# ScalarE's exp stands behind the square of q and the copy of P's transposes

## The chip, the cores and the metric

The kernel runs on one core of a Trainium2 chip. The time is the device time of the core in microseconds, the median of repeated runs. Five engines work side by side, each with its own queue in program order, and wait for each other by semaphores: TensorE (PE in the profile), VectorE (DVE), ScalarE (ACT), GpSimd (POOL) and SyncE (SP), which starts the DMAs.

## The reference, cut to what matters

The input is 16 sequences of 256 tokens with 128 features. A first stage adds a windowed attention with 16 heads of 8. Then come six layers, each an attention and a feed-forward part:

```
for i in range(6):
    x = attn_layer(shift_tokens(x), Wqkv[i], q_scale[i], k_scale[i], Wo[i]) + x
    x = ffn_layer(shift_tokens(x), ln_g[i], ln_b[i], W1[i], b1[i], W2[i], b2[i]) + x

# attn_layer: 16 heads of 64, windows of 32 queries that see 64 keys
q, k, v = split(x @ Wqkv)
q, k = l2norm(q) * qs, l2norm(k) * ksc       # then rotary tables on both
sim = q @ k.T * 8, masked;  attn = softmax(sim);  out = (attn @ v) @ Wo
```

`l2norm` needs the sum of squares of each head of q and k. The softmax needs a row maximum, exp, a row sum and a division.

## The kernel before, in words

After the first stage the six layers run as one software pipeline over blocks of 128 tokens: 32 blocks a layer, 192 in all. In step t every engine does one stage of several blocks at once. Block t (back 0) is projected, squared and rotated. Block t-1 has its q and k transposed and its scores computed. Block t-2 has its maximum, its shift, exp and row sum. Block t-3 has its probabilities P transposed, multiplied with v and projected. Block t-4 is added to x. The feed-forward part of a pair of blocks (a sequence) goes along, split over later steps: `pl.seq(9)` and `pl.seq(11)` act at odd t, `pl.seq(6)` and `pl.seq(10)` at even t. Each engine's order within a step is written out by hand in `step_pe`, `step_act`, `step_dve`, `step_pool` and `step_sp`; nothing reorders it, except that steps of all engines overlap as their semaphores allow.

**TensorE, step t:** q projection into the bank pair `one` (six fp32r matmuls, `q_done`); eight transposes of P of block t-3 into `PC` (waits for `weighed` and for `x_updated` of t-4; `pT_done`); k projection into `other` (`k_done`); eight q transposes of block t-1 into `PC` (wait for `pT_kept`; `qkT_done`); P times v of block t-3 into `PB` (waits for `pT_kept` and `shifted`; `av_done`); eight k transposes of block t-1, into `PC` again (wait for `qkT_kept`, that is for the two copies of qT at L855); v projection; the feed-forward matmuls; scores of block t-1 into `PB`, on top of a mask that VectorE wrote (`masked`); the output projection of t-3.

**ScalarE, step t:** exp of block t-2 in place in `Sx` (L832, waits for `shifted`); square of q into `sq[:, 0]` (L837, waits for `q_done`); copy of P's transposes into `PT` (L840, waits for `pT_done`); square of k into `sq[:, 1]` (L845, waits for `k_done`); at even t a small bias (L850); two copies of qT (L855); oT (L860); kT (L865); VA (L872); then the feed-forward and normalization parts.

**VectorE, step t:** maximum (L998) and shift (L1002) of the scores of t-2; the update of `xT` from t-4 (L1006, `x_updated`); rotation of q in two multiplications (L973, L977; waits for the first `squared`); sums of the squares of q (L981); rotation of k (waits for the second `squared`); the mask for the next scores (L994, waits for `o_kept`, the oT copy); sums of the squares of k; row sums of exp (L1029, waits for `exp_done`) and their reciprocal (L1032); feed-forward parts. GpSimd adds the halves of the rotation (L1101), scales q and k by their norms (L1080) and divides the probabilities (L1112).

At the turn from one layer to the next, VectorE and ScalarE also prepare the next layer's weights and tables. TensorE's projections are interspersed with counts of a semaphore that nobody waits for (`fill`).

Of the kernel before, what the change touches and what calls it, by code (L numbers as in the profile page):

```python
# [9 lines left out]
ACT = mybir.ActivationFunctionType  # L10
# [59 lines left out]
def build(nc, x_in, w_first, wqkv, wo, qkscale, fw1, fw2, vectors, c_rot, c_small, out):  # L70
    ctx = ExitStack()
    with ctx:
        def sb(name, shape, dt=F32):
            return ctx.enter_context(nc.sbuf_tensor(name, shape, dt))

        def sem(name):
            return ctx.enter_context(nc.semaphore(name))
# [38 lines left out]
        Sx = sb("Sx", [P, 2, PAIRS, 2, KEYS])  # L116
# [39 lines left out]
        S = {n: sem(n) for n in (*STEP, *PER_SEQ, *LOADS, *PARTS, *ONCE, *FIRST, "xf0", "xf1", "vb0", "vb1", "vb2", "vb3", "phase",   # L156
                                 "stored", "opened", "o_copied", "o_t", "o_sum", "zeroed",
                                 "cleared", "waited")}
# [48 lines left out]
        A_ = nc.scalar  # L207
# [387 lines left out]
        def blocks(pl, name, back, k):  # L595

            per = STEP[name]
            return pl.times(NBLOCKS * per) + ((pl.t - back) * per + k)
# [57 lines left out]
        def feed_banks(t):  # L656

            other = projections(t)[1]
            return other[:, 0:UNIT], other[:, UNIT:2 * UNIT], PC[:, UNIT:2 * UNIT]
# [165 lines left out]
        def step_act(e, pl):  # L825
            t, r, b, now = pl.t, pl.t % RING, pl.t % BLOCKS, pl.t % 2
            one, other = projections(t)
            bank0, bank1, bank2 = feed_banks(t)
            if pl.has(2):
                e.wait_ge(S["shifted"], blocks(pl, "shifted", 2, 1))  # L830
                rows = Sx[:, now, :, :, :].rearrange("p a w k -> p (a w k)")
                A_.activation(rows, rows, ACT.Exp).then_inc(S["exp_done"], 1)  # L832
            if pl.has(0):
                e.wait_ge(S["q_done"], blocks(pl, "q_done", 0, 1))
                if pl.has(1):
# [2 lines left out]
            if pl.has(3):  # L838
                e.wait_ge(S["pT_done"], blocks(pl, "pT_done", 3, 1))
                A_.activation(PT[:, :, :].rearrange("p a q -> p (a q)"), PC[:, :], ACT.Copy).then_inc(S["pT_kept"], 1)  # L840
            if pl.has(0):
                e.wait_ge(S["k_done"], blocks(pl, "k_done", 0, 1))
                if pl.has(1):
                    e.wait_ge(S["summed"], blocks(pl, "summed", 1, 2))
                A_.activation(sq[:, 1, :], other[:, :], ACT.Square).then_inc(S["squared"], 1)  # L845
# [5 lines left out]
            if pl.has(1):  # L851
                e.wait_ge(S["qkT_done"], blocks(pl, "qkT_done", 1, 1))
                for odd in range(2):
                    rows = slice(odd * DH, (odd + 1) * DH)
# [403 lines left out]
        @block.scalar  # L1258
        def _(act):
            act.wait_ge(S["zeroed"], 1)  # L1260
            A_.preload_act_table_set("natural_log_exp_and_others")
            first = Place(act, 0).at(0)
            act.wait_ge(S["w_loaded"], 16)
            act.wait_ge(S["v_cleared"], 1)
            first_stage(act, first_act)
            meet(act, 1)
            act.wait_ge(S["cleared"], 1)
            for q in range(2):
                round_x(act, first, q)
            steps(act, step_act)  # L1270
            meet(act, 2)
            finish(act, "act")
# [64 lines left out]
```

## Time and profile before

| | |
|---|---|
| median of 3 runs | 3418.71 us (3418.09 to 3419.04) |
| profiled execution | 3418.27 us, span 3416.5 us |
| granted TensorE clock, mean | 0.973 |
| TensorE matmuls busy | 3188.8 us, 93% |
| VectorE busy | 2812.1 us, 82% |
| GpSimd busy | 2626.1 us, 77% |
| ScalarE busy | 2597.2 us, 76% |

Times are microseconds from the start of the span unless marked ns. A row of a timeline gives start, length, engine, line, operation, output from input; in brackets stands the idle time of the engine just before it and what ended it. Lengths of pipelined instructions overlap: the pitch, from start to start, is what a queue pays. The chain of waits is followed back from the last instruction of the kernel: it names, at each moment, the work that everything later waited for.

### The profile page before, as it was taken

Reading aid. Unit: us, or ns where it says so; the run is one execution under the profiler, and the core shown is the slowest. Engines: PE = TensorE matmul, PEld = TensorE weight load, DVE = VectorE, ACT = ScalarE, POOL = GpSimd, SP = SyncE. Lnnn points to the kernel's source line nnn. Section 1 sums busy time; section 2 is a strip of 40 time slices with the busy share of each in tenths; the row PEclk is TensorE's granted clock in tenths of the full one; section 3 lists DMA queues with packets and bytes.
Section 4 is the critical chain, followed back from the end, with each engine's and each line's share of the span. In section 5 each row is a group of like instructions: output and inputs, shape, how many; then the busy total and the mean of one; then the engine's idle time right before and its main releaser. Section 6 shows DMA issues by size and latency. Waiting matters only on the chain.

```text
span 3416.5 us, 133004 instructions
## 1 busy us (share of the span) xinstructions
PE 3188.8 (93%) x52802; PEld 2706.0 (79%) x52802; DVE 2812.1 (82%) x3743; ACT 2597.2 (76%) x3707; POOL 2626.1 (77%) x2593
## 2 busy tenths in 40 slices
PE   7978999989999989999989999989999999999996
PEld 4647888878788878888878888878888878888885
DVE  7967888888788888888888888888878888888882
ACT  6746778877787878778777877878778777878874
POOL 6648888878877878878878878877878887888871
PEclk9979999999999999999999999999999999999997
DMA  1001111111111111111101111111111111111111
GB/s 63 2 10 36 58 39 33 38 28 44 52 43 38 35 31 41 43 56 35 40 27 46 36 58 39 33 33 39 40 59 33 38 35 38 37 40 33 38 35 29
DMA packets 57827, 130.82 MB, mean 38 GB/s; under 512 B 10992, under 2 KB 33136, under 8 KB 56432
## 3 DMA queue, kind: packets, MB, share of 16 engines
q1 hardware_dynamic: 57200, 121.94, 12.2%
q8 instruction: 457, 7.49, 0.9%
q14 instruction: 170, 1.39, 0.1%
HBM read 19.17 MB, written 2.10 MB: 6 GB/s over the span
## 4 chain that ended last, share of the span: by engine, by line
PE 70%; ACT 15%; issue 8%; DVE 5%; POOL 2%; ACTq 0%; DMA 0%; POOLq 0%; DVEq 0%; SPq 0%
PE pair L211 56%; PE pair L214 13%; ACT qT L855 10%; ACT sq L845 3%; DVE ts L977 1%; ACT ss L850 1%; DVE ss L981 1%; DVE mx L998 1%; DVE qk L973 0%; DVE pair L994 0%; DVE tab L955 0%; POOL qk L1080 0%; DVE tab L956 0%; DVE Sx L1002 0%; ACT sq L837 0%
## 5 line engine op out<-in xcount | busy, mean ns | idle before, releaser
L1101 POOL TENSOR_TENSOR qk<-qk,ts 128x1024 f32<-128x1024 f32 x384 | 912.4, 2385 | 228.8 <-DVE ts L977 213.5
L973 DVE TENSOR_TENSOR qk<-pair,tab 128x1024 f32<-128x1024 f32 x384 | 468.2, 1219 | 365.6 <-ACT sq L837 362.8
L1080 POOL TENSOR_TENSOR qk<-qk,rn 128x1024 f32<-128x1024 f32 x384 | 733.1, 1930 | 28.6 <-issue 13.5
L211 PE MATMUL pair<-wq_h,xs_h 128*128 128x512 f32 x1154 | 512.3, 444 | 31.6 <-issue 14.8
L832 ACT ACTIVATE Sx<-Sx 128x1024 f32<-128x1024 f32 x192 | 203.4, 1060 | 395.4 <-DVE Sx L1002 395.4
L214 PE MATMUL pair<-small,qk 128*128 128x128 f32 x3104 | 420.5, 279 | 75.4 <-ACT qT L855 54.5
L1112 POOL TENSOR_TENSOR Sx<-Sx,rden 128x1024 f32<-128x1024 f32 x192 | 365.3, 1902 | 157.2 <-DVE rden L1032 157.2
L211 PE MATMUL pair<-wq_h,xs_l 128*128 128x512 f32 x1152 | 469.7, 408 | 0.4
L211 PE MATMUL pair<-wq_l,xs_h 128*128 128x512 f32 x1152 | 468.4, 407 | 0.0
L977 DVE TENSOR_TENSOR ts<-pair,tab 128x1024 f32<-128x1024 f32 x384 | 466.0, 1214 | 0.0
L981 DVE TENSOR_REDUCE ss<-sq 128x16 f32<-128x1024 f32 x384 | 463.9, 1208 | 0.0
L214 PEld LDWEIGHTS pair<-small,qk 128*128 128x128 f32 x3104 | 338.0, 143 | 154.7 <-issue 106.1
L211 PEld LDWEIGHTS pair<-kT,qT 128*64 128x64 f32 x12288 | 374.4, 138 | 36.2 <-issue 36.2
L211 PE MATMUL pair<-kT,qT 128*64 128x64 f32 x12288 | 400.6, 224 | 2.2 <-DVE pair L994 1.9
L855 ACT ACTIVATE qT<-pair 64x1024 f32<-64x1024 f32 x384 | 389.3, 1014 | 8.0 <-PE pair L214 5.1
L211 PE MATMUL pair<-oT,wo_sb 128*128 128x128 f32 x3072 | 394.5, 282 | 0.0
L211 PE MATMUL pair<-PT,VB 64*64 64x32 f32 x12288 | 375.6, 221 | 5.5 <-issue 3.1
L211 PE MATMUL pair<-PT,VA 64*64 64x32 f32 x12288 | 371.8, 220 | 0.6 <-issue 0.6
L211 PEld LDWEIGHTS pair<-oT,wo_sb 128*128 128x128 f32 x3072 | 358.3, 192 | 12.8
L211 PEld LDWEIGHTS pair<-PT,VB 64*64 64x64 f32 x12288 | 327.5, 135 | 36.5 <-issue 36.4
L211 PEld LDWEIGHTS pair<-PT,VA 64*64 64x64 f32 x12288 | 328.5, 135 | 2.1 <-issue 2.1
L214 PE MATMUL pair<-small,Sx 128*128 128x128 f32 x1792 | 246.5, 283 | 49.2 <-DVE xT L1006 39.7
(126 smaller groups left out, 6678.6 us busy)
## 6 DMA issues: line engine op xcount, KB each, us to landing
VB<-VA SPq DMA_DIRECT2D x192, 384.0 KB, 3.5
VB<-VA SPq DMA_DIRECT2D x96, 128.0 KB, 3.5
wq_raw<-wqkv SPq DMA_DIRECT2D x6, 1536.0 KB, 7.2
xf<-xT SPq DMA_DIRECT2D x96, 64.0 KB, 1.9
xf<-xT SPq DMA_DIRECT2D x96, 63.8 KB, 2.0
wo_sb<-wo SPq DMA_DIRECT2D x6, 512.0 KB, 3.6
X<-x_in SPq DMA_DIRECT2D x4, 512.0 KB, 7.6
out<-X SPq DMA_DIRECT2D x8, 256.0 KB, 2.3
```

The source lines that it names most:

```text
L211: return T_.matmul(out, lhsT, rhs, start=start, stop=stop, **k)
L214: return T_.transpose(out, in_, ident if idn is None else idn)
L832: A_.activation(rows, rows, ACT.Exp).then_inc(S["exp_done"], 1)
L845: A_.activation(sq[:, 1, :], other[:, :], ACT.Square).then_inc(S["squared"], 1)
L850: A_.activation(ss[:, 2 * HEADS:NORMS], f_mv[:, :, 1], ACT.Identity, bias=eps[:, 0:1]).then_inc(S["varied"], 1)
L855: last = A_.activation(qT[rows, :, :, odd * WIN:(odd + 1) * WIN], PC[rows, :].rearrange("p (a w q) -> p a w q", a=PAIRS, w=4), ACT.Copy)
L973: V_.tensor_tensor(h3(qk[:, now, kind, :], DH), h3(source[:, :], DH), rep(tab[:, 2 * kind, b, :], HEADS, DH), ALU.mult)
L977: V_.tensor_tensor(ts[:, kind, :].rearrange("p (h a c) -> p h a c", **halves), swapped, sines, ALU.mult).then_inc(S["rotated"], 1)
L981: V_.tensor_reduce(ss[:, kind * HEADS:(kind + 1) * HEADS], h3(sq[:, kind, :], DH), axis=AX.X, op=ALU.add).then_inc(S["summed"], 1)
L1080: G_.tensor_tensor(x, x, bc(rn[:, then, kind * HEADS:(kind + 1) * HEADS], HEADS, DH), ALU.mult).then_inc(S["scaled"], 1)
L1101: G_.tensor_tensor(qk[:, now, kind, :], qk[:, now, kind, :], ts[:, kind, :], ALU.add).then_inc(S["added"], 1)
L1112: G_.tensor_tensor(x, x, bc(rden[:, now, :], HEADS, KEYS), ALU.mult).then_inc(S["weighed"], 1)
```

## The change: ScalarE's order in a step

The exp of block t-2 moves down by two instructions. ScalarE now squares q first, then copies P's transposes, then does exp, and then squares k. All waits and counts of the semaphores stay as they are, and so does the order of every other engine.

```diff
--- before.py
+++ after.py
@@ -826,10 +826,6 @@
             t, r, b, now = pl.t, pl.t % RING, pl.t % BLOCKS, pl.t % 2
             one, other = projections(t)
             bank0, bank1, bank2 = feed_banks(t)
-            if pl.has(2):
-                e.wait_ge(S["shifted"], blocks(pl, "shifted", 2, 1))
-                rows = Sx[:, now, :, :, :].rearrange("p a w k -> p (a w k)")
-                A_.activation(rows, rows, ACT.Exp).then_inc(S["exp_done"], 1)
             if pl.has(0):
                 e.wait_ge(S["q_done"], blocks(pl, "q_done", 0, 1))
                 if pl.has(1):
@@ -838,6 +834,10 @@
             if pl.has(3):
                 e.wait_ge(S["pT_done"], blocks(pl, "pT_done", 3, 1))
                 A_.activation(PT[:, :, :].rearrange("p a q -> p (a q)"), PC[:, :], ACT.Copy).then_inc(S["pT_kept"], 1)
+            if pl.has(2):
+                e.wait_ge(S["shifted"], blocks(pl, "shifted", 2, 1))
+                rows = Sx[:, now, :, :, :].rearrange("p a w k -> p (a w k)")
+                A_.activation(rows, rows, ACT.Exp).then_inc(S["exp_done"], 1)
             if pl.has(0):
                 e.wait_ge(S["k_done"], blocks(pl, "k_done", 0, 1))
                 if pl.has(1):
```

## Rows read from the trace of the kernel before

**Rows 1.** The page: busy time and share of each engine; the chain by line.

```profile
PE 3188.8 (93%) x52802; PEld 2706.0 (79%) x52802; DVE 2812.1 (82%) x3743; ACT 2597.2 (76%) x3707; POOL 2626.1 (77%) x2593
...
PE pair L211 56%; PE pair L214 13%; ACT qT L855 10%; ACT sq L845 3%; DVE ts L977 1%; ACT ss L850 1%; DVE ss L981 1%; DVE mx L998 1%; DVE qk L973 0%; DVE pair L994 0%; DVE tab L955 0%; POOL qk L1080 0%; DVE tab L956 0%; DVE Sx L1002 0%; ACT 
```

**Rows 2.** The chain in order of time (start, length, what), 1500 to 1535.

```profile
1507.93 1.43 PE pair L211 x6
...
1509.46 1.02 ACT sq L845
...
1511.40 1.03 ACT qT L855
...
1512.57 1.07 PE pair L214 x8
...
1516.78 5.39 PE pair L211 x86
```

**Rows 3.** The table of waits: us in total, times, the longest.

```profile
DVE qk L973 <- ACT sq L837: 362.8, 192, 6.7
...
PE pair L214 <- ACT qT L855: 54.5, 189, 2.2
...
PE pair L214 <- DVE xT L1006: 39.7, 6, 8.0
```

**Rows 4.** ScalarE's timeline, 1500 to 1535: start, length, line, operation.

```profile
1507.20 1.00 ACT L837 ACTIVATE sq<-pair 128x1024 f32<-128x1024 f32 x1
1508.11 1.02 ACT L840 ACTIVATE PT<-pair 128x1024 f32<-128x1024 f32 x1
1509.46 1.02 ACT L845 ACTIVATE sq<-pair 128x1024 f32<-128x1024 f32 x1 [0.34 <-PE pair L211]
...
1512.45 1.03 ACT L860 ACTIVATE oT<-pair 128x1024 f32<-128x1024 f32 x1
...
1521.83 1.06 ACT L832 ACTIVATE Sx<-Sx 128x1024 f32<-128x1024 f32 x1 [2.19 <-DVE Sx L1002]
1522.80 1.01 ACT L837 ACTIVATE sq<-pair 128x1024 f32<-128x1024 f32 x1
1523.70 1.01 ACT L840 ACTIVATE PT<-pair 128x1024 f32<-128x1024 f32 x1
1524.87 1.03 ACT L845 ACTIVATE sq<-pair 128x1024 f32<-128x1024 f32 x1 [0.16 <-PE pair L211]
```

**Rows 5.** TensorE's timeline, the same stretch.

```profile
1506.66 0.39 PE L211 MATMUL pair<-wq_l,xs_h 128*128 128x512 f32 x1
1506.89 1.03 PE L214 MATMUL pair<-small,Sx 128*128 128x128 f32 x8
...
1508.95 0.40 PE L211 MATMUL pair<-wq_l,xs_h 128*128 128x512 f32 x1
...
1521.78 0.39 PE L211 MATMUL pair<-wq_l,xs_h 128*128 128x512 f32 x1
1522.23 1.09 PE L214 MATMUL pair<-small,Sx 128*128 128x128 f32 x8
...
1524.33 0.43 PE L211 MATMUL pair<-wq_l,xs_h 128*128 128x512 f32 x1
```

**Rows 6.** VectorE's timeline, the same stretch.

```profile
1508.24 1.23 DVE L973 TENSOR_TENSOR qk<-pair,tab 128x1024 f32<-128x1024 f32 x1 [1.84 <-ACT sq L837]
...
1513.90 1.22 DVE L994 COPY pair<-small 128x1024 f32<-128x1024 f32 x1
...
1521.71 0.28 DVE L1006 TENSOR_TENSOR xT<-pair,xT 128x128 f32<-128x128 f32 x1
```

**Rows 7.** Weight loads in time, 1686 to 1688.

```profile
1687.20 0.19 PEld L211 LDWEIGHTS pair<-f_h,w_h 128*128 128x128 f32 x1 [0.45 <-issue]
```

**Rows 8.** The chain in order of time, 1262 to 1269, at a layer turn.

```profile
1264.80 2.29 PE pair L211 x6
```

**Rows 9.** Busy time by stretch (count), then PEclk, DMA share, GB/s.

```profile
50.00:100.00 50.00, 45.57 (x566) 30.47 (x564) 47.12 (x109) 37.74 (x102) 34.93 (x80) 1.00 0.01 2
```

## The prediction

> **What bounds the kernel now.** I began with the page: TensorE is the busiest engine at 93%, and in the chain of waits its two lines hold 56% and 13% [rows 1]. So TensorE sets the pace, with one detour through ScalarE: qT L855 is 10% of the chain and sq L845, the square of k, 3%. VectorE, busy for 82%, has no line above 1% in it.
>
> The chain in order of time shows that detour [rows 2]. TensorE ends the k projection, ScalarE squares k (from 1509.46), then makes the two qT copies, and only then does TensorE start the k transposes at 1512.57. The table of waits says the same of nearly every block: TensorE waited for qT 189 times [rows 3]. It shows only 54.5 us for this, but a wait that sits in the chain matters by being last, not by its length: whatever makes qT later makes TensorE later by as much.
>
> Then I laid out a pair of blocks from the timelines, one odd t (first instruction of the changed region at 1507.20) and one even t, and measured everything from Q, the end of the q projection. For the odd block Q = 1506.66 + 0.39 = 1507.05, for the even one 1521.78 + 0.39 = 1522.17 [rows 5].
>
> - Odd block: square of q at Q + 0.15, P copy at Q + 1.06, square of k at Q + 2.41 [rows 4]. The k projection ends at 1508.95 + 0.40 = 1509.35, Q + 2.30 [rows 5]. So the square of k starts 0.11 after its matmuls end: nothing but that latency holds it.
> - Even block: exp at 1521.83, square of q at Q + 0.63, P copy at Q + 1.53, square of k at Q + 2.70 [rows 4], with the k projection ending at 1524.33 + 0.43 = 1524.76, Q + 2.59 [rows 5]. Again 0.11 of latency.
>
> In both, ScalarE reaches the square of k with time to spare, because exp ran ahead of Q, while ScalarE had nothing else to do. VectorE waits too, 1.84 us before its rotation [rows 6] and 362.8 us in all [rows 3], for the square of q. That wait looks like the prize of this change, but VectorE hardly stands in the chain.
>
> **The change, part by part.** No instruction is added or removed; 192 exps move past the square of q and the P copy, and land right before the square of k. No DMA is moved, and nothing on TensorE, VectorE or GpSimd changes its place. Two new queueing relations arise: exp now waits behind q_done and pT_done, and the square of k waits behind exp.
>
> The square of q. It waits for q_done alone and starts at about Q + 0.11 (the latency seen at the square of k). Gain: 0.04 in the odd block, 0.52 in the even one. It goes to VectorE's rotation and to the P copy.
>
> The P copy. It comes 0.91 after the square of q (1507.20 to 1508.11 [rows 4]), so at Q + 1.02. In the odd block the transposes of P run from 1506.89 for 1.03 and are done by Q + 0.87 [rows 5]: in time. In the even block they start 0.45 after the last q matmul instead of 0.23 [rows 5], right after VectorE's xT update, which runs from 1521.71 for 0.28 [rows 6]. VectorE gains 0.5 on TensorE here (below), so I take this 0.22 gap as closed, and the copy at Q + 1.02 too.
>
> exp. The pair "P copy, then exp" doesn't stand in this trace. Bounds: a pitch of 0.91, that of the square of q and the P copy, and 1.05 if nothing overlaps, as from the second qT copy at 1511.40 [rows 2] to oT at 1512.45 [rows 4]. Two pairs overlap by 0.09: the square of q lasts 1.00 with a pitch of 0.91, exp lasts 1.06 with a pitch of 0.97. So I take 1.02 - 0.09 = 0.93 for the P copy, nearest to them in shape and line: exp at Q + 1.95.
>
> The square of k. It follows an exp by 0.97 (1521.83 to 1522.80 [rows 4]): Q + 2.92. Its matmuls end at Q + 2.30 in the odd block and, with the gap closed and the P copy earlier, near that in the even one. So exp is now what it waits for, in both blocks. It is later by 2.92 - 2.41 = 0.51 in the odd block and 2.92 - 2.70 = 0.22 in the even one. Other even blocks, read in the same way, have it up to Q + 2.81, and there 0.11 is lost. I use 0.18 as the mean.
>
> Behind it on ScalarE stand qT (both halves), oT, kT and VA. qT goes straight into TensorE's wait for the k transposes, so all of TensorE's later work in the block (k transposes, v projection, feed-forward part, scores, output projection, next q projection) moves by the same 0.51 or 0.18. oT is needed by VectorE's mask copy at 1513.90, Q + 6.85 [rows 6]. oT begins at Q + 5.40 now [rows 4]; at Q + 5.91 and 1.03 long it holds the mask until about Q + 7.0, some 0.15 late. But the scores, which read it, follow the short transposes at 1516.78, Q + 9.7 [rows 2], so the mask stays covered, and VectorE still gains about 0.5 - 0.15 on TensorE in the odd block: this closes the 0.22 gap of the even one. exp's own readers lose nothing: the row sums stand behind the mask in VectorE's order, and the mask starts 4 us after exp's new end.
>
> The sum. The first blocks have no P copy or exp, and at the five layer turns the k projection runs at half clock, 2.29 us for its six matmuls instead of 1.43 [rows 8, 2], which covers exp. That leaves about 95 odd blocks at 0.51 = 48.5 and 88 even ones at 0.18 = 16: 64.5 us. Some even blocks have stalls in TensorE's own stream after the k transposes: weights that wait 0.45 for "issue" [rows 7]. I take a part, 3 us, as absorbed there, since a longer wait ahead of them may let the queue fill. Total +61.
>
> The profiled execution took 3418.27 us, span 3416.5, and the median of the runs is 3418.71. They agree within 0.5, so I add the sum to the median: 3480 us.
>
> **Rivals.**
>
> *Half of the move (faster).* If TensorE could use the earlier P copy and the square of q, the even block would lose its 0.22 gap and about 0.2 ahead of the q transposes (they start 0.53 after the last k matmul there, 0.32 in the odd block). Up to 0.4 x 90 = 36 us faster, 3383. This needs exp to fit in before the k projection ends, that is, the projection would have to end at Q + 2.80 or later. For it: VectorE's 362.8 us of waiting. Against: it ends at Q + 2.30 in the odd block. 4%.
>
> *Hidden anyway (same).* If TensorE's wait for qT weren't last, or the later stalls of its queue absorbed 0.2 to 0.5 in each block, the time would stay at 3419. Against: the chain passes through qT in both blocks, and odd blocks show no such stall behind it. 4%.
>
> *Worse bounds (slower still).* No overlap between P copy and exp (+0.12 x 183 = 22), and the even block's 0.22 gap stays because it is TensorE's queue and not xT (+0.22 x 88 = 19): 3480 + 41 = 3521; either alone gives about 3500. 17% for something near both, 3505 to 3525.
>
> *The clock.* The longer stall, up to 0.8 us per block where 54.5 / 189 = 0.29 stands now [rows 3], might cost TensorE its clock. The granted clock is 1.00 (of 2.4 GHz) from 50 to 100 us, where TensorE is busy 45.57 of 50 us, 91% [rows 9]. It was at 1.2 GHz behind the one long wait of a turn, 8.0 us for xT [rows 3, 8]. After the change TensorE would be busy 3189 of some 3478 us, 92%: above that first stretch. If in a fifth of the blocks the k transposes and the v projection, 1.07 and about 1.4 us, took twice as long, that is 0.2 x 2.5 x 192 = 96 us more, 3576. The Trainium skill's "TensorE: Matmul & The Clock Gate", section on psum-queue depth-cycling, reports a kernel whose micro-idles between groups of matmuls made the clock oscillate; by that rule this rival would come true. The trace of before has short idles in every block and the full clock over the stretch of [rows 9], so it doesn't agree so far. 3%.
>
> **How the numbers follow.** Forecast 72%, worse bounds 17%, clock 3%, faster 4%, same 4%. A difference of 0.2% (7 us) is about what can be told from no change. Most of the range is the forecast's own bounds. It goes down to 3456, where the start latency is 0.07 instead of 0.11, the even blocks lose nothing and the turns give back about half of VectorE's 1.84 (-7, -13, -4), and up to 3508, which takes in either of the worse bounds alone. Slower 0.92, same 0.04, faster 0.04.
>
> **What would show it.** After the change: exp at Q + 1.95, the square of k at Q + 2.9 in both blocks with a releaser on ScalarE itself instead of the k projection; TensorE's wait for qT up from 54.5 to about 54.5 + 60 and more (up to 120, since the closed gaps reappear there); VectorE's wait before L973 for sq L837 down, but idle before L998 (for the scores) up; the xT-bound gap in even blocks gone; ScalarE idle before L837 instead of before exp. The prediction is wrong if the square of k still starts 0.11 after its matmuls, or if the odd block's period, 15.12 us from Q to Q now, doesn't grow by about 0.5.

## The result and the profile after

The changed kernel takes 3478.4 us (median of 4 runs, 3475.05 to 3483.91) against 3418.88 before: a ratio of 1.0173, 95% interval 1.0156 to 1.0191. It is slower by about 59.5 us; 3480 was forecast, with 3456 to 3508 as the range. The profiled execution took 3475.05 us, its span is 3473.3.

The page's chain, by line:

```profile
PE pair L211 50%; ACT qT L855 10%; PE pair L214 9%; ACT sq L845 5%; ACT sq L833 5%; ACT PT L836 5%; ACT Sx L840 2%; ACT ss L850 1%; DVE wq_l L963 0%; DVE tab L955 0%; POOL sq L399 0%; DVE VB L321 0%; POOL wq_l L963 0%; DVE qk L317 0%; DVE m
```

Three ScalarE instructions are new in it: sq L833 (the square of q), PT L836 (the P copy) and Sx L840 (exp). Before, the chain touched ScalarE only from the square of k on [rows 2]; now the whole row from the square of q to qT stands in it. The chain in order of time, in an odd block:

```profile
1555.30 1.03 ACT sq L833
1556.33 0.92 ACT PT L836
1557.24 0.30 ACT Sx L840
...
1558.07 1.02 ACT sq L845
1559.10 0.89 ACT qT L855
```

ScalarE's timeline, an even block and the odd one behind it:

```profile
1538.93 1.03 ACT L833 ACTIVATE sq<-pair 128x1024 f32<-128x1024 f32 x1 [2.65 <-PE pair L211]
1539.91 1.03 ACT L836 ACTIVATE PT<-pair 128x1024 f32<-128x1024 f32 x1
1540.97 1.06 ACT L840 ACTIVATE Sx<-Sx 128x1024 f32<-128x1024 f32 x1
1541.94 1.01 ACT L845 ACTIVATE sq<-pair 128x1024 f32<-128x1024 f32 x1
...
1555.30 1.03 ACT L833 ACTIVATE sq<-pair 128x1024 f32<-128x1024 f32 x1 [2.09 <-PE pair L211]
1556.22 1.02 ACT L836 ACTIVATE PT<-pair 128x1024 f32<-128x1024 f32 x1
1557.12 1.06 ACT L840 ACTIVATE Sx<-Sx 128x1024 f32<-128x1024 f32 x1
1558.07 1.02 ACT L845 ACTIVATE sq<-pair 128x1024 f32<-128x1024 f32 x1
```

TensorE's, the same stretch:

```profile
1538.43 0.39 PE L211 MATMUL pair<-wq_l,xs_h 128*128 128x512 f32 x1
1538.79 1.09 PE L214 MATMUL pair<-small,Sx 128*128 128x128 f32 x8
...
1545.20 1.06 PE L214 MATMUL pair<-small,qk 128*128 128x128 f32 x8 [0.84 <-ACT qT L855]
...
1554.79 0.39 PE L211 MATMUL pair<-wq_l,xs_h 128*128 128x512 f32 x1
...
1557.08 0.40 PE L211 MATMUL pair<-wq_l,xs_h 128*128 128x512 f32 x1
...
1561.16 1.06 PE L214 MATMUL pair<-small,qk 128*128 128x128 f32 x8 [0.71 <-ACT qT L855]
```

In the odd block Q = 1554.79 + 0.39 = 1555.18. The square of q starts at Q + 0.12, the P copy at Q + 1.04, exp at Q + 1.94, the square of k at Q + 2.89, though its matmuls ended at Q + 2.30. Against [rows 4] that is 0.48 later. In the even block Q = 1538.82: Q + 0.11, 1.09, 2.15 and 3.12, where the square of k stood at Q + 2.70. TensorE's idle before the k transposes, 0.23 to 0.24 before, is 0.71 and 0.84 now. Over all blocks the medians for the square of k are Q + 2.89 (2.40 before) in odd blocks and Q + 3.12 (2.75 before) in even ones. The odd block's period, which was to grow by about 0.5 from 15.12, is 15.59 in the block before this one (Q = 1523.23 to 1538.82): 0.47 more.

The table of waits, against [rows 3]:

```profile
ACT sq L833 <- PE pair L211: 494.6, 191, 8.3
DVE qk L973 <- ACT sq L833: 336.1, 187, 6.8
...
PE pair L214 <- ACT qT L855: 139.6, 190, 2.2
```

TensorE waits 85 us more for qT. VectorE's wait for the square of q shrank by only 27 us, from 362.8: its rotation can start no earlier than TensorE's q projection allows, and it now waits for oT too. The 395.4 us that ScalarE used to idle ahead of exp are 494.6 us of idling ahead of the square of q: the room in which exp ran unseen is still there, and nothing stands in it.

By blocks, from one kT copy to the next on ScalarE's timeline: the 164 steady blocks (from t = 12 on, without the blocks around the turns) take 63.6 us more, 0.39 each; the 15 blocks at the turns 2.3; the first 12 together 0.1. The first stage, in which no instruction differs, happened to be 6.4 shorter, and the end 2.7. Together 56.8, the difference of the spans.

### The profile page after: what moved, and what is told of

Its sections match the earlier page's. It is cut to its first block, busy times and chain, and to the rows that moved or that the text cites. A ratio compares the mean times of both kernels' runs of the same rounds, so it can differ in the third digit from the quotient of the medians.

```text
span 3473.3 us, 133004 instructions
## 1 busy us (share of the span) xinstructions
PE 3169.9 (91%) x52802; PEld 2700.4 (78%) x52802; DVE 2829.9 (81%) x3743; ACT 2586.7 (74%) x3707; POOL 2625.7 (76%) x2593
## 4 chain that ended last, share of the span: by engine, by line
PE 59%; ACT 29%; issue 7%; DVE 3%; POOL 1%; ACTq 0%; DMA 0%; DVEq 0%; POOLq 0%; SPq 0%
PE pair L211 50%; ACT qT L855 10%; PE pair L214 9%; ACT sq L845 5%; ACT sq L833 5%; ACT PT L836 5%; ACT Sx L840 2%; ACT ss L850 1%; DVE wq_l L963 0%; DVE tab L955 0%; POOL sq L399 0%; DVE VB L321 0%; POOL wq_l L963 0%; DVE qk L317 0%; DVE mx L998 0%
## 5 line engine op out<-in xcount | busy, mean ns | idle before, releaser
L833 ACT ACTIVATE sq<-pair 128x1024 f32<-128x1024 f32 x192 | 196.9, 1025 | 494.6 <-PE pair L211 494.6
L214 PE MATMUL pair<-small,qk 128*128 128x128 f32 x3104 | 419.6, 278 | 155.9 <-ACT qT L855 139.6
L211 PEld LDWEIGHTS pair<-wq_h,xs_h 128*128 128x128 f32 x1154 | 222.6, 193 | 74.9 <-issue 26.7
```

What stands on the lines that cost most here:

```text
L211: return T_.matmul(out, lhsT, rhs, start=start, stop=stop, **k)
L214: return T_.transpose(out, in_, ident if idn is None else idn)
L833: A_.activation(sq[:, 0, :], one[:, :], ACT.Square).then_inc(S["squared"], 1)
```

## Experiments

Ratios are against the kernel before on the same chip, whose median was 3414.74 us in the first four runs, 3420.5 in the next four, 3416.62 in the last four. Orders name ScalarE's instructions of a step: q and k for the squares, P for the copy, E for exp; before is E q P k qT oT kT VA, after is q P E k qT oT kT VA. Q is the end of the q projection throughout. Two theories stood at the start: mine, that an instruction costs by what TensorE waits for behind it (here qT); and that exp being late, or VectorE's order of waits, costs by itself. The diffs are shortened: words in place of code stand for one ScalarE instruction or more, "..." for what is left out. Where a median over blocks is given for an experiment, it is that of the steady blocks of its profiled execution, 89 odd and 83 even ones from t = 15 on, without the even blocks at the turns.

**1. exp one place up (q E P k).**

```diff
             (square of q)
+            exp of t-2
             (copy of P)
-            exp of t-2
             (square of k)
```

> ScalarE's order is square of q, exp, copy of P, square of k: exp moves one place up from the changed kernel. The square of k should stand at Q + 2.9 as in the changed kernel. My theory (TensorE waits for qT, and qT waits for whatever stands before it or for the q transposes, which need the P copy): P copy from Q + 1.1 to about Q + 2.0, the q transposes start at its end + 0.14 = Q + 3.15 and end at Q + 4.2, qT can start only then, some 0.45 later than in the changed kernel: 3478 + 0.42 x 180 = about 3553 us. Rival (only that exp stands somewhere ahead of the square of k counts): 3478, no change.

Measured 3548.06 us, ratio 1.039 (1.0373 to 1.0407). The chain in time, odd block, from the square of q:

```profile
1553.43 1.02 ACT sq L833
1554.46 0.95 ACT Sx L837
1555.41 0.92 ACT PT L840
...
1556.46 1.08 PE pair L214 x8
...
1557.57 1.02 ACT qT L855
...
1559.76 1.06 PE pair L214 x8
```

The square of k starts at 1556.21 with Q = 1552.92 + 0.40 = 1553.32, the same Q + 2.9 as after, yet the kernel is some 70 us slower. The P copy holds the q transposes, these hold qT, which starts at Q + 4.25, 0.46 later than in the changed kernel. So it isn't the square of k as such, nor exp's distance from it: it is when qT can start.

**2. exp behind the square of k (q P k E qT).**

```diff
             (square of k)
+            exp of t-2
             (bias L850, even blocks)
             (copies of qT)
```

> Order square of q, copy of P, square of k, exp, qT. The square of k goes back to 0.11 after the k projection (Q + 2.4 odd, Q + 2.6 to 2.7 even). My theory (qT's start is what counts): exp now holds qT by its whole pitch of 0.97 with no slack ahead to absorb it, so 3419 + 0.97 x 95 + 0.9 x 88 less 10 for the turns = about 3575 to 3590 us. Rival (the late square of k itself costs, through VectorE's rotation of k and the sums): 3410 to 3419 us.

Measured 3655.16 us, ratio 1.0706 (1.0688 to 1.0724). ScalarE, odd block (qT follows at 1634.66):

```profile
1632.79 1.02 ACT L841 ACTIVATE sq<-pair 128x1024 f32<-128x1024 f32 x1 [0.35 <-PE pair L211]
1633.71 1.05 ACT L845 ACTIVATE Sx<-Sx 128x1024 f32<-128x1024 f32 x1
```

The square of k is back at 0.1 after its matmuls and the time is the worst of all: the rival is out. But 240 us is 69 to 84 more than the 156 to 171 that I expected. TensorE's idle for qT is mostly 1.18 to 1.44 a block here, and behind some of these idles the clock falls: cut into 140 stretches of 20 us from 400 to 3200, the trace has 58 with a granted clock below 1.00; before there are 15, after 14. Summed as (1 - clock) x 20 us, what is missing to full clock is 112 us here, 39 before and 41 after: some 71 us more than after, about the size of the excess. The next run shows the same effect coming in.

**3. A small copy ahead of the square of k, in both kernels.**

```diff
+            if pl.has(0):
+                A_.activation(junk[:, :], small[:, 0:256], ACT.Copy)
             if pl.has(0):
                 e.wait_ge(S["k_done"], ...)
```

> The changed kernel with one more ScalarE copy of 128x256 into a tile that nobody reads, right before the square of k (pitch about 0.33 to 0.40 by the small copies of this kernel). My theory: no slack is left there, so every block pays it whole: 3478 + 0.36 x 183 = 3540 to 3550 us. Rival (the time came from somewhere else, VectorE's new order of waits or TensorE's queue, and ScalarE still has slack before the square of k): 3478 to 3485 us.

> The same copy at the same place in the kernel before. There the slack before the square of k is 2.41 - (1.06 + 0.93) = 0.42 in odd blocks and 2.70 - (1.53 + 0.93) = 0.24 in even ones. My theory: odd blocks pay nothing, even ones about 0.1: 3419 to 3432 us. Rival (any work added to ScalarE costs its length): 3419 + 66 = 3485 us.

Measured in the changed kernel 3559.85 us, ratio 1.0411 (1.0386 to 1.0437): 81 us more than without it. In the kernel before 3418.06 us, ratio 1.0014 (1.0003 to 1.0025): 3 to 5 us. ScalarE in the kernel before with the copy, an odd block:

```profile
1540.37 1.02 ACT L841 ACTIVATE PT<-pair 128x1024 f32<-128x1024 f32 x1
1541.28 0.42 ACT L843 ACTIVATE junk<-small 128x256 f32<-128x256 f32 x1
1541.72 1.03 ACT L848 ACTIVATE sq<-pair 128x1024 f32<-128x1024 f32 x1
```

and in the changed one:

```profile
1565.47 1.06 ACT L841 ACTIVATE Sx<-Sx 128x1024 f32<-128x1024 f32 x1
1566.41 0.41 ACT L843 ACTIVATE junk<-small 128x256 f32<-128x256 f32 x1
1566.72 1.02 ACT L848 ACTIVATE sq<-pair 128x1024 f32<-128x1024 f32 x1
```

The copy, 0.42 long, just fits ahead of the square of k in the first and pushes it by its pitch of 0.31 in the second. The same work at the same place costs next to nothing in one order and all of its pitch in the other; that is the slack that the change used up. Its 81 us are more than 0.31 x 183 = 57. The rest sits in blocks where TensorE ran at 1.2 GHz: 32 of the 140 stretches are below 1.00, and by the same sum 70 us are missing to full clock, 28 more than after. Such a block:

```profile
1551.96 1.66 PE L215 MATMUL pair<-small,qk 128*128 128x128 f32 x8 [1.19 <-ACT qT L858]
...
1553.84 0.63 PE L212 MATMUL pair<-wq_h,xs_l 128*128 128x512 f32 x1
1554.27 0.63 PE L212 MATMUL pair<-wq_l,xs_h 128*128 128x512 f32 x1
```

Eight k transposes take 1.66 instead of 1.06, and the fp32r matmuls stand 0.43 apart instead of 0.23, right behind an idle of 1.19. Counted over all blocks, no such group was slow behind the 153 waits for qT of 0.6 to 0.9 us in the changed kernel; with the copy added 9 of 131 were behind idles of 0.9 to 1.1, and in the run of experiment 2 13 of 93 behind 1.1 to 1.3 and 33 of 83 behind longer ones.

**4. exp further down, where ScalarE has time: behind kT, oT, VA.** exp is gone from its place ahead of the square of q in all three.

```diff
             (copies of qT)
             (copy oT)         + exp here: behind oT
             (copy kT)         + exp here: behind kT
             (copy VA)         + exp here: behind VA
```

> Order square of q, copy of P, square of k, qT, oT, kT, exp, VA: exp goes where ScalarE waits for the v projection anyway (0.45 idle), and nothing of TensorE's next waits stands behind it but VA. My theory: the square of k is back at 0.11 after the k projection, Q + 2.4 odd and about Q + 2.6 even (2.75 before), exp ends at about Q + 8.6 (odd) and Q + 9.1 (even), just ahead of VectorE's row sums; the turns keep their 2 us each: 3415 - 9 - 10 = about 3395 to 3405 us, faster than both. Rival (exp late is what costs, through row sums and division): 3430 us and more.

> exp between oT and kT. The square of k and qT as in the run with exp behind kT, but kT ends about 0.75 later, Q + 8.4 in odd blocks, and there TensorE's transposes of xf into the same bank wait for it (they start at Q + 7.8 in the kernel before). My theory (each instruction's place is priced by the wait of TensorE that stands behind it): odd blocks lose about 0.6, even ones nothing: 3400 + 57 = 3455 us or so. Rival (only work ahead of qT costs): 3400 us.

> exp behind VA, at Q + 9.1 to 9.6, ending at Q + 10.1 to 10.6. VectorE's row sums stood at Q + 9.1 before and now wait for it, about 1.0 to 1.5 a block, and VectorE has some 1.7 us of waiting per block elsewhere, but its maximum for the next block comes late. My theory: VectorE's lateness reaches TensorE through x_updated at the next transposes of P, 0.3 to 0.8 a block: 3450 to 3550 us. Rival (VectorE's slack swallows it): 3400 us.

Measured: behind kT 3428.61 us, ratio 1.0026 (1.0016 to 1.0037); behind oT 3496.98 us, 1.0235 (1.022 to 1.0251); behind VA 3546.89 us, 1.0379 (1.0363 to 1.0396).

Behind kT 50 of the 59 us are back, with exp later still. From the table of waits of that run:

```profile
DVE hid L1066 <- ACT hid L894: 125.8, 103, 9.7
...
DVE den L1029 <- ACT Sx L865: 8.6, 2, 7.6
```

VectorE's row sums waited for exp only twice, so being late isn't what costs there, though the rival's 3430 us is nearer than my 3400. It isn't faster than before either, and three other things differ, whose shares I didn't separate. In an even block VectorE's xT update ends at 1523.19, the transposes of P start at 1523.43, 0.46 after the last q matmul, and the square of k stands at Q + 2.72: the gap of 0.22 is back, because VectorE gains on TensorE only when TensorE is slower. In 50 of the 83 even blocks xT sets the start in this way, and the median for the square of k is Q + 2.71, not the 2.6 that I expected. Next, the bias L850 follows the square of k by 1.05 in even blocks, where it was 0.92 before, and qT starts at Q + 3.96 (3.84 before, medians). And the gelu parts stand behind exp on ScalarE now: VectorE waits 125.8 us for them (63.9 before), and in 37 of the 89 odd blocks the transposes of P start late, behind xT, which happened in none before.

Behind oT the chain goes through kT, as expected, and costs more than I worked out:

```profile
1504.56 0.22 ACT Sx L861
...
1505.40 1.03 ACT kT L865
...
1506.57 0.41 PE pair L214 x2
```

kT from 1505.40 ends at 1506.43, and TensorE's transposes of xf follow 0.14 later. From kT to kT, against the kernel before, odd blocks take 0.72 more (57.5 us for 80 of them; 0.6 was expected), and a part of the even blocks another 22.6 us, which I did not follow up. Behind VA exp's lateness itself is on the path, through VectorE's row sums and on to xT, as I expected (3450 to 3550 us), and VectorE's slack doesn't swallow it. Its table of waits:

```profile
DVE den L1029 <- ACT Sx L873: 246.8, 192, 8.0
...
PE pair L214 <- DVE xT L1006: 132.3, 138, 5.4
```

VectorE waits 246.8 us for exp, TensorE 132.3 us for xT (39.7 before).

**5. Fewer counting instructions between TensorE's matmuls, in even blocks.** The transposes of P in even blocks start 0.36 after the last q matmul in the changed kernel, with xT ready at 1537.97 + 0.28 = 1538.25, 0.54 ahead.

```diff
-        FILL = (43, 21, 46, 21, 44, 22, 47, 21, 46, ...)
+        FILL = (21, 21, 21, 21, 21, 22, 21, 21, 21, ...)
```

> The changed kernel, in which the counting instructions strewn over TensorE's projections are about 21 in every block, where even blocks had 39 to 48. In the changed kernel the transposes of P in even blocks start 0.36 to 0.39 after the last q matmul although xT was ready 0.5 before; in odd blocks 0.23. If TensorE's instruction queue makes this gap (my theory now), it falls to 0.23, the P copy comes 0.1 earlier, exp overlaps it as in odd blocks, and the square of k goes from Q + 3.12 to Q + 2.89 in even blocks: 3478 - 0.23 x 85 = about 3458 us. Rival (the gap has another cause): no change, 3478; moved fetches of instructions at the loop's turn may add or take a few us in either case.

Measured 3473.84 us, ratio 1.0169 (1.0153 to 1.0184), not to be told from the changed kernel's 1.0173. An even block on TensorE:

```profile
1539.86 0.40 PE L211 MATMUL pair<-wq_l,xs_h 128*128 128x512 f32 x1
1540.10 1.03 PE L214 MATMUL pair<-small,Sx 128*128 128x128 f32 x8
```

and on ScalarE:

```profile
1541.29 1.02 ACT L836 ACTIVATE PT<-pair 128x1024 f32<-128x1024 f32 x1
1542.34 1.06 ACT L840 ACTIVATE Sx<-Sx 128x1024 f32<-128x1024 f32 x1
```

The gap is gone, as my theory said: 0.24 in this block, at most 0.26 in 71 of the 83 even blocks, and 0.23 in the median, where the changed kernel has 0.37. So the counts made it. But the gain of 20 us didn't follow, for two reasons. exp still starts 1.05 after the P copy and not 0.90, so the square of k comes at Q + 3.05 (median; 3.12 in the changed kernel, 2.89 expected). And the counts aren't idle decoration: TensorE now stops for about 0.8 us of "issue" in the middle of the matmuls of P with v in 40 blocks, 4 in the changed kernel. The period of even blocks fell from 16.48 to 16.35 (medians), while that of odd ones rose from 15.60 to 15.69 (means).

**6. The bias L850 (even blocks, pitch 0.19) moved from ahead of qT to ahead of kT, in three kernels.**

```diff
             (square of k)
-            (bias L850)
             (copies of qT)
             (copy oT)
+            (bias L850)
             (copy kT)
```

> The changed kernel with the small bias of even blocks (L850, pitch 0.19) moved from ahead of qT to between oT and kT, where ScalarE idles 0.19. My theory (in the changed kernel ScalarE's row from the square of q to qT is the chain, with no gap): even blocks win 0.19, 3478 - 0.19 x 85 = about 3462 us. Rival (ScalarE has room before qT): 3478 us.

> The same move in the kernel before. There the q transposes end at Q + 3.78 in even blocks and qT starts at Q + 3.81, so qT would wait for TensorE instead: my theory says 3415 to 3420 us, no change. Rival (the whole row ahead of qT is the chain there too): 3420 - 16 = 3404 us.

> The run with exp behind kT, with the bias moved too. There the q transposes end at about Q + 3.6 in even blocks, qT starts at Q + 3.97: the move can win 0.3 a block: 3428 - 0.3 x 85 = about 3403 us, which would be faster than the kernel before by 0.4%. Rival (what made that run slower than 3400 lies behind the k transposes): 3425 us.

Measured: in the changed kernel 3465.59 us, ratio 1.0139 (1.0124 to 1.0155), by the ratios 12 us less than without the move, with intervals that just touch, and the period of even blocks fell by 0.14 (medians 16.48 and 16.34); in the kernel before 3420.63 us, 1.0009 (1.0 to 1.0018), nothing won; with exp behind kT 3417.24 us, 0.9998 (0.9989 to 1.0007), 10 us less by the ratios, not the 25 that I expected. The first two are the pair of experiment 3 with the sign turned: taking 0.19 away from ScalarE's row pays where the row is the chain, and not where it has slack.

The third is level with the kernel before, not faster. VectorE and TensorE at its even to odd seam:

```profile
1529.29 1.26 DVE L1066 SCALAR_TENSOR_TENSOR hid<-pair,vec_b,hid 128x256 f32<-128x256 f32 x3 [1.11 <-ACT hid L894]
...
1532.86 0.28 DVE L1006 TENSOR_TENSOR xT<-pair,xT 128x128 f32<-128x128 f32 x1
```

```profile
1533.05 0.39 PE L211 MATMUL pair<-wq_l,xs_h 128*128 128x512 f32 x1
1533.38 1.09 PE L214 MATMUL pair<-small,Sx 128*128 128x128 f32 x8
```

exp ahead of VA delays VA and with it, on ScalarE, the table load and the gelu parts of even blocks. VectorE waits 1.11 for them, its xT update ends at 1533.14, and the odd block's transposes of P start 0.24 after that, 0.33 after the last q matmul instead of 0.23. 38 of the 89 odd blocks start them late, none before. Against the kernel before, the period of even blocks is 0.09 shorter (medians 16.05 and 15.96) and that of odd ones 0.10 longer (15.11 and 15.21): what the even block wins, the odd one gives back.

**7. The square of q one place down (E P q k).**

```diff
             exp of t-2
-            (square of q)
             (copy of P)
+            (square of q)
             (square of k)
```

> Order exp, copy of P, square of q, square of k: the kernel before with the square of q one place down. The square of k then stands at about Q + 2.8 odd and Q + 3.1 even, as in the changed kernel, but the square of q comes at Q + 1.9 to 2.2 instead of Q + 0.11. If TensorE's wait for qT alone sets the price and VectorE's 1.7 us of waiting is slack: 3478 us. My theory now: VectorE has 11.1 us of work between its rotation and its maximum in an odd block, it would end 1.8 later, more than its slack, and TensorE would wait for xT: 3600 us or more.

Measured 3584.64 us, ratio 1.0488 (1.0472 to 1.0504), far from 3478 and somewhat under my figure. VectorE's waits:

```profile
DVE qk L973 <- ACT sq L840: 655.2, 192, 6.7
...
PE pair L214 <- ACT qT L855: 114.3, 179, 2.2
...
PE pair L214 <- DVE xT L1006: 87.2, 86, 2.1
```

VectorE's wait for the square of q grows from 362.8 to 655.2 us. TensorE's rise for qT is only 60 us of the 168; it now also waits for xT in 86 places, 6 before, as I expected. In even blocks the transposes of P start 1.40 after the last q matmul (0.45 before), and they hold the P copy and with it the squares: the square of q stands at Q + 3.05 and that of k at Q + 3.95 there, far behind the 3.1 that I expected, so these blocks aren't those of the changed kernel with a late square of q alone. So the square of q can't be late; no run here shows a gain from its being early.

## Why the prediction was right

**The mechanism.** The runs bear it out: TensorE waits for qT behind a row of ScalarE's work, exp filled an idle stretch ahead of Q, and moved behind Q it used up the slack ahead of the square of k (0.42 in odd blocks, 0.24 in even ones) and then pushed qT. qT came 0.47 later in odd blocks (Q + 3.79, 3.32 before) and 0.36 later in even ones (4.20, 3.84 before). Experiment 3 shows the slack, 1 and 2 show that qT's start counts and not the square of k, 4 that exp's lateness does not count until it meets the row sums.

**Odd blocks, 0.51 forecast.** The square of k came at Q + 2.89, forecast Q + 2.92. Start latency 0.12 (0.11), q to P 0.92 (0.91), P to exp 0.90 (0.93), exp to k 0.95 (0.97).

**Even blocks, 0.18 forecast: too small.** The square of k came at Q + 3.12, not 2.92, so 0.37 later than its median before. The step that failed is "I take this 0.22 gap as closed". VectorE gained what I worked out, xT was ready 0.5 ahead, yet the gap shrank only from 0.45 to 0.36. And the P copy and exp don't overlap there: 1.06 from start to start, the "no overlap" bound of the range, where odd blocks have 0.90. Experiment 5 shows what I had wrong: xT was one bound of that gap, and the counting instructions of even blocks, which the sum put at nothing, were the next one, at 0.37 in the median. With fewer of them the gap is 0.23. Why exp doesn't overlap the P copy in even blocks stays open.

**What evened it out.** The terms at 0.49 and 0.37 would make 0.43 a block; measured were 0.39 in steady blocks. A part is absorbed behind the k transposes, as forecast, in even blocks that already had "issue" stalls behind the v projection: the block that held such a stall of 0.45 [rows 7] reaches its scores at Q + 11.35, the same as Q + 11.32 before, and the plain even block of [rows 5] at Q + 10.90, 0.39 later. Two blocks show this; I did not sort all of them. The 15 blocks at the turns cost 2.3 us in all, where 0.39 each would be 5.9: TensorE's waits for xT fell from 39.7 to 30.6 us, but those for the next layer's rounded weights (wq_l L963) rose from 6.6 to 14.6, so most of what the turns seemed to give back was only moved. And the first stage and the end were 9 us shorter in this profile without any edit to them. So 3480 against 3478.4 is closer than its terms deserve: that a term too small and several small savings cancelled to within 2 us is luck.

**Signs that were forecast.** TensorE's wait for qT rose to 139.6 us, above the 120 named as its upper end; the even blocks cost more than forecast. The odd block's period grew by 0.47, close to the 0.5 named. The gap of even blocks no longer ends with xT, but it isn't gone. VectorE's idling moved, but ahead of the mask (12.8 to 49.8 us) and of the gelu parts, not ahead of the maximum as I wrote: that one stayed at TensorE's pace.

**The rivals.** *Half of the move* and *hidden anyway* needed ScalarE to have room ahead of the square of k; the copy of experiment 3 shows that there was room for about 0.4 in odd blocks before and that there is none now. *Worse bounds*: in even blocks the P copy and exp don't overlap, and more than half of the gap of 0.22 stayed, on TensorE's side and not for xT (experiment 5); neither holds in odd blocks. *The clock* didn't come at idles such as 0.71 and 0.84 us, in none of the 153 blocks with 0.6 to 0.9; it is real behind some of the larger ones (experiments 2 and 3). The stretch of [rows 9] that I held against it lies in the first stage, ahead of the six layers, so its full clock said nothing on the short idles of the pipeline. Within the layers, 1300 to 1440 of the kernel before has a granted clock of 1.00 too. The rule of the Trainium skill that I cited for it, "TensorE: Matmul & The Clock Gate" on psum-queue depth-cycling, is borne out by these two runs and not by the changed kernel, where 14 of the 140 stretches were below 1.00 against 15 before.

## What to carry to other kernels

Ask of each instruction on a helper engine what the bound engine waits for behind it, and how long its queue idles ahead of that wait; work that sits in an idle stretch is free if nothing that others wait for is held up behind it (behind kT exp did hold something up), and moving it behind the event that ends the stretch costs its pitch less the slack that is left. A large wait of an engine that isn't the bound (VectorE's 362.8 us) is no prize. A short dummy instruction at the disputed place, put into both kernels, shows directly whether there is slack of its size. And look at more than one block before saying what an experiment did to a gap: in the run with fewer counts, 12 of 83 even blocks still have it.

## What the runs showed of the hardware that I had not expected

- TensorE's granted clock falls to 1.2 GHz behind some idles and not behind others of the same length. Of the groups of eight k transposes, 0 of 153 were slow behind idles of 0.6 to 0.9 us in the changed kernel and 0 of 115 in the run of experiment 7; 9 of 131 behind 0.9 to 1.1 with the copy added; 13 of 93 behind 1.1 to 1.3 and 33 of 83 behind longer ones with exp ahead of qT. In the block of experiment 3 the clock is back by the end of the v projection. Missing to full clock from 400 to 3200: 39 us before, 41 after, 36 with exp between q and P (which is 70 us slower than after, with idles of 0.87 and 0.23 in the block shown in place of one), 70 with the copy added, 112 with exp ahead of qT. So a long wait can be paid a second time, in the clock.
- Two ScalarE instructions of one kind, a copy from PSUM and then exp, stood 0.90 apart in odd blocks and 1.05 to 1.06 in most even ones. In the changed kernel the copy had mostly waited for its transposes there. That isn't the cause: with fewer counts (experiment 5) it followed the square of q by 0.93 or less in 78 even blocks, and in 72 of these exp was still 1.04 or more behind it. The same kind of difference stands between the square of k and the bias L850, 0.92 before and 1.05 with exp behind kT. What decides it stays open.
